# Loading and projecting the second layer's context inside the first mixture of experts, and the short last tile of the second mixture on four column tiles

## What is computed

```python
# layer 0, mixture: 8 experts, each token goes to its best two
down = einsum('eti,ehi->eth', silu(x @ w_gate) * (x @ w_up), w_down)     # L0_ffn
# layer 1, decay: a scan over time, a product, and a depthwise convolution of 5 taps
y = einsum('tbd,ed->tbe', S, W) + b + conv(x)                            # L1_attn
# layer 1, cross attention: keys and values come from the context, not from x
kh, vh = ctx @ Wk, ctx @ Wv;  out = softmax(qh kh^T / sqrt(d), causal) vh @ Wo + bo   # L1_xattn
# layer 2, mixture: 8 experts, at most C = 538 tokens each
h = gelu(buf @ W1 + b1);  y = h @ W2 + b2                                # L2_ffn
```

## Time and profile before

| | |
|---|---|
| median of three runs | 2727.8 us (2727.51 to 2731.99) |
| profiled execution, its own time | 2732.52 us |
| its span, first to last instruction | 2731.2 us |
| mean granted TensorE clock | 0.933 |
| PE busy | 2386.4 us (87%) |
| DVE busy | 1175.9 us (43%) |
| ACT busy | 895.6 us (33%) |
| POOL busy | 569.6 us (21%) |
| DMA, mean over the span | 82 GB/s |

### The profile page before, as it was taken

How to read it: one execution, slowest core, us unless ns; L and a number is a source line. 1 busy time by engine, 2 the same in 40 slices (tenths; PEclk the granted TensorE clock), 3 DMA queues, 4 the chain that set the end, 5 groups by cost and what they waited for, 6 DMA issues and landing times. The chain is left out here.

```text
span 2731.2 us, 33181 instructions
## 1 busy us (share of the span) xinstructions
PE 2386.4 (87%) x13065; PEld 1621.3 (59%) x13086; DVE 1175.9 (43%) x2251; ACT 895.6 (33%) x2428; POOL 569.6 (21%) x567
## 2 busy tenths in 40 slices
PE   6786999938997998887999999599976899889999
PEld 5674777726775655223566657477752588644555
DVE  5643222266787554564333311300016466755220
ACT  2211222232773543553222221222213465414220
POOL 1621222225001012012343410222212100132100
PEclk9877999969999999998999999699987899989999
DMA  4006888630001002100000000323215633100000
GB/s 162 0 32 250 300 309 301 253 114 1 2 2 51 1 1 90 39 1 31 1 0 0 1 1 1 132 90 92 86 57 223 280 140 140 57 10 1 8 8 16
DMA packets 75378, 224.15 MB, mean 82 GB/s; under 512 B 9359, under 2 KB 52757, under 8 KB 65238
## 3 DMA queue, kind: packets, MB, share of 16 engines
q1 hardware_dynamic: 67894, 204.76, 20.5%
q0 software_dynamic: 7328, 17.26, 1.8%
HBM read 178.61 MB, written 45.17 MB: 82 GB/s over the span
## 5 line engine op out<-in xcount | busy, mean ns | idle before, releaser
L221 PE MATMUL psum<-arena 128*128 128x256 f32 (+6 forms) x4095 | 1046.1, 412 | 19.7 <-ACT arena L2962 4.0
L221 PEld LDWEIGHTS psum<-arena 128*128 128x128 f32 (+2 forms) x4100 | 723.5, 184 | 296.9 <-issue 131.1
L263 POOL TENSOR_SCALAR x_moments<-x_moments 128x4 f32<-128x4 f32 x48 | 12.0, 251 | 866.6 <-DVE x_moments L256 866.1
L1898 DVE TENSOR_REDUCE small<-psum 128x4 f32<-128x1024 f32 (+1 forms) x112 | 137.1, 1224 | 114.9 <-PE psum L1809 64.2
L1234 POOL DMA_INDIRECT l_out<-arena,slot_tables x79 | 78.9, 998 | 442.2 <-ACT arena L1407 232.7
L3386 PE MATMUL psum<-arena 128*128 128x512 bf16 x752 | 165.4, 379 | 0.8
L1871 ACT ACTIVATE arena<-psum,small 128x128 f32<-128x128 f32 (+1 forms) x384 | 149.1, 414 | 51.2 <-DVE small L1898 51.2
L1426 DVE TENSOR_TENSOR arena<-arena,psum 128x352 f32<-128x352 f32 x78 | 40.7, 522 | 252.6 <-ACT arena L1385 252.6
L1909 DVE COPY arena<-psum 128x512 f32<-128x512 f32 x224 | 143.7, 681 | 1.7 <-PE psum L1820 1.5
L1804 PE MATMUL psum<-arena 32*128 32x128 f32 (+1 forms) x1280 | 132.6, 338 | 0.0
L2832 POOL TENSOR_TENSOR small<-small,minus_half 128x16 f32<-128x16 f32 x32 | 92.9, 2903 | 179.4 <-DVE small L2746 179.4
(11 more groups left out here) (340 smaller groups left out, 3381.3 us busy)
## 6 DMA issues: line engine op xcount, KB each, us to landing
arena<-L_ffn_w_in SPq DMA_DIRECT2D x39, 2176.0 KB, 8.8
arena<-L_ffn_W_in SPq DMA_DIRECT2D x16, 1024.0 KB
positions<-arena SPq DMA_DIRECT2D x16, 1024.0 KB, 6.1
arena<-positions SPq DMA_DIRECT2D x16, 1024.0 KB, 8.1
arena<-l_out SPq DMA_DIRECT2D x16, 512.0 KB, 7.4
positions<-arena SPq DMA_DIRECT2D x16, 512.0 KB, 6.6
arena<-positions SPq DMA_DIRECT2D x16, 512.0 KB, 9.3
arena<-ctx_in SPq DMA_DIRECT2D x2, 2048.0 KB, 10.1
```

Of the source, the lines that this page charges most:

```text
L221: last = nc.tensor.matmul(out, lhsT, rhs, start=(n == 0), stop=(n == len(pairs) - 1))
L1898: nc.vector.reduce_max(self.minus_top(h), use.bank(u).rearrange("p (h l) -> p h l", l=L), AX_X, negate=True).then_inc(self.topped.up(), 1)
```

## The change

**Context, loads.** The context's fetch is split. `ctxT` now lies in slab 0 (under the first weight buffer), `Wk` and `Wv` at the end of slab 3 (under the fourth). In `L0Mixture.sp` the decay's weights are issued after block 35's output, and `ctxT`, `Wk`, `Wv` after block 36's. `Wq`, `Wo` and the bias row (`fetch_rest`) stay where the context's loads were, at the start of the decay stage.

**Context, work.** PE forms all keys right after the last block's output, three pairs of values before the transposes of group 0 and five before those of group 1. ACT first waits for the scatters, then empties the keys, and the pairs between its parts of the norm. POOL's clearing of the value buffer follows the last scatter. In the decay stage PE has only transposes and the eight outputs, which now lie in banks 0 to 7 in order.

**Second mixture.** The last tile of an expert is no longer a sum of eight products into 26 partitions. `pe_strips` forms it first, over the last 32 tokens: product m of eight goes to partitions 32s to 32s+31 of one bank, s = m // 2, so that four partial sums stand under each other. ACT copies them out, and after the four full tiles one product with a matrix of four stacked identities (`same_row`, made once by POOL) adds them up into 26 partitions.

```diff
@@ L0Mixture
+        self.context = k.context = L1Context(k, u)
...
-        self.finals("pe")
+        for g in range(GROUPS):
+            self.context.keys.pe(g, [(self.context.fetch.loaded,)])
+        for g in range(GROUPS):
+            for n in self.context.pairs_before(g):
+                self.context.pairs.pe_pair(n)
+            self.next.norm.pe_final(g)
...
-        self.finals("act")
+        for stored in self.y_stored:
+            act.wait_ge(stored)
+        for g in range(GROUPS):
+            self.context.keys.act(g)
+        for g in range(GROUPS):
+            for n in self.context.pairs_before(g):
+                self.context.pairs.empty_pair(n, "act", (self.context.cleared,))
+            self.next.norm.act_final(g)
...
+        self.context.pool()
         self.finals("pool")
...
+        sp.wait_ge(*self.uses.filled(self.y_use[BLOCKS - self.RING]))
+        self.next.fetch.sp()
+        sp.wait_ge(*self.uses.filled(self.y_use[BLOCKS - self.RING + 1]))
+        self.context.fetch.sp()
         self.sp_combine(k.l0_out)
@@ L1Context
+    def pairs_before(self, g):
+        return ((), (), (0, 1, 2), (3, 4, 5, 6, 7))[g]
@@ L1Decay.pe
-        for g in range(GROUPS):
-            self.context.keys.pe(g, [(self.context.fetch.loaded,)])
         for n, u in enumerate(self.out):
-            self.context.pairs.pe_pair(n)
             pe.wait_ge(self.state_in, n // 2 + 1)
@@ L1Decay.pool
-        self.context.pool()
@@ L1Decay.sp
-        self.context.fetch.sp()
+        self.k.context.fetch_rest.sp()
@@ L2Mixture.pe
-            for a, u in enumerate(self.y_use[e]):
-                n = self.count(a)
-                products(nc, use.take(u)[0:n, 0:D], [(self.hid[e % 2][:, m, P * a:P * a + n], w2[:, m, :])
-                                                     for m in range(MT)]).then_inc(use.fills(u), 1)
+            self.pe_strips(e)
+            for a, u in enumerate(self.y_use[e][:-1]):
+                products(nc, use.take(u)[:, 0:D], [(self.hid[e % 2][:, m, P * a:P * a + P], w2[:, m, :])
+                                                   for m in range(MT)]).then_inc(use.fills(u), 1)
+            u, n = self.y_use[e][-1], self.count(self.RT - 1)
+            pe.wait_ge(self.folded)
+            pe.wait_ge(*use.emptied(self.strip_use[e]))
+            nc.tensor.matmul(use.take(u)[0:n, 0:D], self.same_row[:, 32 - n:32], self.strips[e % 2],
+                             start=True, stop=True).then_inc(use.fills(u), 1)
+    def pe_strips(self, e):
+        nc, use, u, per = self.k.nc, self.uses, self.strip_use[e], self.MT // 4
+        bank = use.take(u)
+        for j in range(per):
+            for s in range(4):
+                mm = nc.tensor.matmul(bank[32 * s:32 * s + 32, 0:D], self.hid[e % 2][:, per * s + j, CAPACITY - 32:CAPACITY],
+                                      self.w2[e % 2][:, per * s + j, :], start=(j == 0), stop=(j == per - 1))
+        mm.then_inc(use.fills(u), 1)
@@ L2Mixture.act, after each expert's Gelus and turned rows
+            copied(k, "act", self.strips[e % 2], use.bank(u)[:, 0:D]).then_inc(use.empties(u), 1)
```

More of the change, by code:

```diff
@@ L1246, in sp_combine @@
                                     rows[:, rank, 4 * g:4 * g + 4, :]).then_inc(self.fetched[g].up(), 16)
-        self.next.fetch.sp()
     def dve_combine(self):
@@ L1499, in __init__ @@
         self.pairs = PairValues(k, uses, self.v, self.wv, self.ctxT, 0)
+        for g in range(GROUPS):
+            self.keys.use.append([uses.add("act", 1, DC * g + c) for c in range(DC)])
+        for n in range(TILES // 2):
+            self.pairs.use.append(uses.add("act", 1, n % 6))
         self.cleared = k.counter("values_cleared", "pool").reserve(1)
+    def pairs_before(self, g):
+        return ((), (), (0, 1, 2), (3, 4, 5, 6, 7))[g]
     def done(self):
@@ L1520, in __init__ @@
         u = self.uses = Uses(k)
-        self.context, self.out = L1Context(k, u), []
-        k.context = self.context
-        for g in range(GROUPS):
-            self.context.keys.add(("act", "act"))
-        for n in range(TILES // 2):
-            self.context.pairs.add("act")
-            self.out.append(u.add("dve"))
+        self.out = [u.add("dve") for _ in range(TILES // 2)]
         u.close()
@@ L1585, in act @@
         for g in range(GROUPS):
-            self.context.keys.act(g)
-        for n in range(TILES // 2):
-            self.context.pairs.empty_pair(n, "act", (self.context.cleared, 1))
-            if n % 2:
-                self.next.norm.act_final(n // 2)
+            self.next.norm.act_final(g)
     def dve(self):
@@ L1948, in __init__ @@
         context = self.context = k.context
-        self.fetch = context.fetch
+        self.fetch = context.fetch_rest
         self.norm = Norm(k)
@@ L2891, in __init__ @@
         self.router = Router(k, u, self.norm, self.fetch.loaded, E * RT, CAPACITY, False)
-        self.turn_use, self.h_use, self.y_use = [[u.add("dve", 2), u.add("act", 2)]], [], []
+        tail = k.arena[:, 4 * SLAB + 2 * 4352 + E * D:4 * SLAB + 2 * 4352 + E * D + 2 * D + 32]
+        self.strips, self.same_row = [tail[:, D * n:D * n + D] for n in (0, 1)], tail[:, 2 * D:]
+        self.folded = k.counter("same_row_made", "pool").reserve(1)
+        self.turn_use, self.h_use, self.y_use, self.strip_use = [[u.add("dve", 2), u.add("act", 2)]], [], [], []
         for e in range(E):
@@ L2896, in __init__ @@
                 self.turn_use.append([u.add("dve", 2), u.add("act", 2)])
+            self.strip_use.append(u.add("act"))
             self.y_use.append([u.add("dve") for _ in range(RT)])
@@ L2964, in act @@
             self.empty_turn(e + 1, "act")
+            u = self.strip_use[e]
+            act.wait_ge(*use.filled(u))
+            if e >= 2:
+                act.wait_ge(*use.filled(self.y_use[e - 2][-1]))
+            copied(k, "act", self.strips[e % 2], use.bank(u)[:, 0:D]).then_inc(use.empties(u), 1)
         self.finals("act")
@@ L2994, in pool @@
     def pool(self):
-        pool = self.k.pool
+        k, pool = self.k, self.k.pool
+        rows = [k.ident[:, 32 * s:32 * s + 32] for s in range(4)]
+        pool.step(k.nc.gpsimd.tensor_tensor(self.same_row, rows[0], rows[1], ALU.add))
+        pool.step(k.nc.gpsimd.tensor_tensor(self.same_row, self.same_row, rows[2], ALU.add))
+        k.nc.gpsimd.tensor_tensor(self.same_row, self.same_row, rows[3], ALU.add).then_inc(self.folded.up(), 1)
         self.load_rows(0)
         self.load_rows(1)
-        pool.wait_ge(self.k.zeroed)
+        pool.wait_ge(k.zeroed)
         for e in range(E):
```

20 lines of the change are left out of this document (11 added, 9 removed).

## The result

| | before | changed |
|---|---|---|
| median, first measurement | 2727.66 us (4 runs) | 2701.47 us (4 runs) |
| ratio, 95% interval | | 0.9903, 0.9887 to 0.9918 |
| median, repeat (run e9) | 2728.3 us (11 runs) | 2701.93 us (6 runs) |
| ratio, 95% interval | | 0.9911, 0.9895 to 0.9927 |
| profiled execution, its own time | 2732.52 us | 2702.26 us |

The kernel is faster by 26 us. I had forecast 20.4, and the time lies just under my range.

A forecast was written before the change was run, and what follows sets the result against it. PE, busy 87% of the span, was taken as the bound, with DVE's chain binding around the rows' return. First layer -6.0 and second mixture -14.4 gave -20.4: 2727.8 to 2707.4 us, range 2702 to 2717.

The forecast's parts named there:

- all later stages only shift: Behind the first layer's decay stage: queries, attention and later stages move earlier by the same 6.0 us, with no further gain.
- the price of the tails: Second mixture: old narrow tile costs 3.75 us, strips and their sum 1.95; gain 1.8 per expert, 14.4 for eight.
- the clock behind the pauses: Decay stage's end: outputs 6 and 7 take 7.2 us, not 5.2, after PE's pauses; +2.0, leaving a 6.0 us gain.
- Cause and place: Predicted profile marks: keys without a DMA wait, decay stage near 588, taps near 605.7, last add 647 to 653, strips 1.0 to 1.2.
- Keys and pairs cost nothing: During the rows' return: PE's context work hides beside DVE's chain at no cost, with cover some 1.3 us deep.
- The clearing, -3.5: Decay stage: moving POOL's MEMSET earlier frees DVE's two-column factor, 3.70 us down to 0.19; gain 3.5 us.
- 0.2 us or so that I charged for each change of shape: Second mixture: each switch between wide and narrow tiles on PE was priced at about 0.2 us extra.
- Rival 1: Decay stage: outputs 6 and 7 run at 1.2 GHz throughout, 10.4 us; gain 2.8 + 14.4, time 2710.6 us; chance 0.17.
- Rivals 2 to 4: Strips overlap only in pairs, 2713.0 us, chance 0.13; context lands late, 2711.4, 0.05; strips run singly with drains, 2752.2, 0.03.

The follow-up runs named there:

- e9: The changed kernel itself, run again unaltered beside the kernel before: 2701.93 us (6 runs), ratio 0.9911.
- e12: The changed kernel with ten unread products of 256 columns on PE behind the context's keys: 2710.65 us (one run).
- e3: The changed kernel with POOL also clearing 6144 unused columns in the decay stage, where the clearing ran before: median 2709.78 us.
- e7: The changed kernel with ten unread products of 256 columns on PE behind output 5 of the decay stage: 2703.3 us (five runs).
- e8: The changed kernel with the second mixture's strips done twice over: 2707.62 us (one run).
- e13: The kernel before with eight unread products in each of two PE pauses of the mixture of depths: 2726.06 us against 2729.89, ratio 0.9982.
- e11: The changed kernel with the strips in the other order, both products of a column tile behind one another: 2697.4 us (one run).
- e5: The changed kernel with outputs 6 and 7 of the decay stage in banks 0 and 1: 2704.37 us (one run).
- e6: The changed kernel with outputs 6 and 7 in banks 0 and 1 and ahead of the transposes of groups 0 and 1: 2699.47 us (4 runs).
- e10: The same kernel as e6, run again beside the changed kernel: 2698.58 us (4 runs), ratio to before 0.9895.

## Why the prediction was right and wrong

My sum was -20.4, and -26.2 and -26.4 were measured. The way was right and the size was not: two steps of the sum failed, that all later stages only shift (5.4 us, 0.7 of them in layer 3) and the price of the tails (1.7), and a smaller one worked the other way (the clock behind the pauses, 0.7).

- **Cause and place: right.** All marks that I named came, to 0.5 us: keys without a wait, decay stage near 588, factor 0.17 us, taps at 605.60, output 6 behind DVE's copy, last add at 650.17, strips 1.00 us. Only the expert's period fell by 2.0 us and not by 1.8.
- **Keys and pairs cost nothing: right** (e12: with 4.3 us more of them it was 1.1).
- **The clearing, -3.5: right** (A 3.53; e3).
- **The clock behind the pauses, +2.0: too small.** Outputs 6 and 7 took 8.2 us at first hand where I took 7.2; the gain of this stage was 5.3 (A and C) instead of 6.0. By the rule of the Trainium skill that I had set beside it ("TensorE: Matmul & The Clock Gate", section "HAM oscillation — how this bites in real kernels"), who leaves gaps pays half rate behind them; e7 agrees with it, 5.3 us with the gap filled and 8.2 with it open.
- **The mixture's tail, -1.8 per expert: too small.** Old tail: 2.01 + 1.54 = 3.55 us, where I had 3.75. New tail: 1.00 + 0.54 = 1.54, where I had 1.95. The step that failed is the 0.2 us or so that I charged for each change of shape, on top of the distances between starts: e8 leaves 0.13 for all that the strips add beside their overlap, and the sum over the partials takes 0.54 with its two changes, where I had 0.44 + 0.3. What a change costs the wide records beside it, 0.2 us on the four full tiles, stood in both kernels, and I counted a part of it a second time beside the old tail's 3.55. The page "TensorEngine Tiling (Array Packing)" of the Trainium skill (section "Tiling Modes") has such a change drain TensorE; the traces fit that, with 0.31 us for the record ahead of it instead of 0.216, and none shows that it is the drain. Gain 2.0 per expert, 16.1 us for eight and 16.8 to 17.0 with what layer 3 adds, not 14.4.
- **"Queries, attention and all later stages hang on the same z and shift by the same": wrong, and the largest miss.** I had put the clock of the later stages at nothing, without a reason. E and F give another 4.7 us. The records of these stages are the same, and PE is busy with them for less time (198.14 and 194.91 us in E), because they meet full clock at other places; e13 gets as much with fillers alone. Why a shift of some 5 us moves the slow spells just so stays open.
- **Rival 1** (half clock through both outputs, 2710.6) did not come true, though half clock lasted longer than I had reckoned, to within the row at 647.04: the outputs took 8.2 us, nearer to my 7.2 than to its 10.4. Rivals 2 to 4 are out (e8, e11; no wait for the context).

In sum -5.3 - 4.7 - 16.8 = -26.8 by the columns, -26.2 and -26.4 by the medians, against my -20.4. That these agree so well is in part luck: single executions of one kernel lie up to 12 us apart (e9).

## What to carry to other kernels

A stage that ends a few microseconds earlier does not simply shift what comes behind it. Where PE pauses for some microseconds, the products behind may run at 1.2 or 2.4 GHz, and a shift can change which; here that gave the changed kernel 4.7 us, and in the traces of e3, e5 and e12 column D alone took back 4 to 5. Forecast such terms with a band of some 5 us and compare several edits before blaming one for it. Where PE must wait, first look for useful work to pull into the pause (the outputs in e6), and if there is none, unread products are not absurd: in e7 and e13 they made their own stage shorter. And take a second execution of each kernel before explaining a difference of 0.2%: of the first pair of traces' difference some 3 to 4 us (3.3 in column H) were late Gelus that did not come again.

## What the runs showed of the hardware that I had not expected

- Strips of 32 columns overlap perfectly for as much as there are (0.87 us for sixteen records of 256 columns, a quarter of the full tiles' time), whatever their order: 1.00 or 1.02 us.
- Putting in one more row of narrow records costs 0.13 us beside the records themselves. The wide records next to a narrow tile take 0.31 and 0.32 us instead of 0.216, in both kernels.
- A POOL clearing of 6144 columns holds a two-column DVE instruction for 3.70 us instead of 0.17, each time it was tried. The two-column TENSOR_TENSOR just ahead of it, which also starts beside the clearing, still takes its 0.16 us; why the one is held and the other not, no run here tests.
- ACT can fall behind for no visible reason: up to 1.65 us before a Gelu instead of 0.42, in six experts of one execution of before (0.8 us of PE for each of the fullest), and never in experts 1 to 7 of any other execution. What it was stays open; the change was not tried for it.
- The first cross attention (D) took 193.0 to 194.1 us in nine executions, at a granted clock of 0.97, and 196.6 to 199.4 in seven, at 0.93 to 0.95, with e10 and e6, the same kernel, on different sides. So the clock makes the difference; what decides on which side an execution falls stays open.
